# Self attention's weight preparation moved into the tile network's routing: a blind prediction and its test

## The reference, cut to what matters

```python
q = where(signatures_raw > 0.3, 1, where(signatures_raw < -0.3, -1, 0))
cluster_idx = argmax(calibrate(xf @ cluster_sigs.T, knots, temperature))
local_idx   = argmax(of the tile gates inside the chosen cluster)
comp = tanh(gelu(xf @ compress_w1 + compress_b1) @ compress_w2 + compress_b2)
```

```python
Q = (x @ Wq.T + bq)   # K and V alike; Wq is 1024 x 128
scores = Q K^T * (64 ** -0.5 * adaptive_scale) ; w = softmax(scores)
y = x + ((w V) @ Wo.T + bo)
y = (y - mean(y)) / sqrt(var(y) + 1e-5) * gamma + beta
```

## Time and profile before

| what | us |
|---|---|
| median of 3 runs | 1909.03 |
| the runs | 1909.03, 1908.49, 1919.20 |
| the profiled execution's own time | 1915.3 |
| its span, first to last instruction | 1913.4 |
| tile network's first matmul | at 997.81 |
| tile network's last write of xT ends | at 1135.48 |
| first projection of self attention | at 1150.75 |
| first scores of self attention | at 1170.50 |

### The profile page before, as it was taken

One profiled execution on the slowest core, in us unless ns is written; L12 is line 12 of the kernel. 1 busy time (PEld: TensorE's weight loads), 2 busy tenths in 40 slices (PEclk: granted clock), 3 DMA queues, 4 the chain that ended last, 5 costly groups with the idle time before them and its releaser, 6 DMA issues. The chain is left out here.

```text
span 1913.4 us, 28911 instructions
## 1 busy us (share of the span) xinstructions
PE 1666.6 (87%) x10515; PEld 952.9 (50%) x10515; DVE 1266.2 (66%) x1719; ACT 1204.2 (63%) x2565; POOL 478.5 (25%) x396
## 2 busy tenths in 40 slices
PE   5999999999999865888776878999999999589976
PEld 2344444444343322666654534656666666356655
DVE  2777777777777729798727444566666666388864
ACT  3787777777777624788862344555655556267764
POOL 2111011111111105777610001222222223145540
PEclk9999999999999955899985678999999999789997
DMA  3000000000000021000000000000000000000001
GB/s 127 1 12 1 1 6 24 0 0 0 0 0 1 0 47 30 5 5 8 2 2 0 1 0 1 1 1 1 1 1 1 1 1 1 7 8 8 2 1 45
DMA packets 30529, 16.99 MB, mean 9 GB/s; under 512 B 8545, under 2 KB 29246, under 8 KB 30398
## 3 DMA queue, kind: packets, MB, share of 16 engines
q1 hardware_dynamic: 27710, 10.52, 2.1%
q10 hardware_dynamic: 2688, 4.72, 0.7%
HBM read 13.14 MB, written 2.10 MB: 8 GB/s over the span
## 5 line engine op out<-in xcount | busy, mean ns | idle before, releaser
L2090 POOL TENSOR_TENSOR self_probs<-self_probs,self_rz 128x1024 f32<-128x1024 f32 x64 | 121.4, 1897 | 516.9 <-DVE self_rz L2118 516.9
L536 POOL TENSOR_SCALAR gru_decay<-gru_zgate 128x512 f32<-128x512 f32 x96 | 75.5, 786 | 570.0 <-ACT gru_zgate L489 544.0
L2065 ACT ACTIVATE self_probs<-self_scores,self_neg 128x128 f32<-128x128 f32 x512 | 181.8, 385 | 16.6 <-DVE self_neg L2113 16.6
L402 PE MATMUL gru_gate<-gru_xn,gru_whg 128*128 128x512 f32 x384 | 182.5, 598 | 3.5 <-DVE gru_xn L582 3.5
L406 PE MATMUL gru_hid<-gru_xn,gru_whg 128*128 128x512 f32 x384 | 181.3, 594 | 0.0
L414 PE MATMUL gru_out<-gru_y,gru_wo 128*128 128x512 f32 x384 | 178.1, 599 | 0.7 <-DVE gru_y L610 0.7
L1235 ACT ACTIVATE x_pt<-x_turned 77x512 f32<-77x512 f32 x256 | 137.4, 586 | 62.1 <-PE x_turned L1126 60.8
L1126 PE MATMUL x_turned<-const_ident,x_probs 128*77 128x128 f32 x1024 | 142.8, 283 | 24.0 <-POOL x_probs L1284 12.5
L1126 PEld LDWEIGHTS x_turned<-const_ident,x_probs 128*77 128x77 f32 x1024 | 115.3, 150 | 76.3 <-POOL x_probs L1284 27.1
L605 DVE SCALAR_TENSOR_TENSOR gru_ghid<-gru_hid,gru_half_c,gru_sighid 128x512 f32<-128x512 f32 x96 | 71.8, 747 | 114.8 <-ACT gru_sighid L490 114.6
L1359 DVE TENSOR_REDUCE x_m<-x_scores 128x16 f32<-128x1232 f32 x64 | 91.5, 1430 | 45.8 <-PE x_scores L1115 40.8
(11 more groups left out here) (377 smaller groups left out, 3567.9 us busy)
## 6 DMA issues: line engine op xcount, KB each, us to landing
gru_whg<-in_L_attn_Whg ACTq DMA_DIRECT2D x4, 768.0 KB, 9.2
x0e_ctx_in<-in_ctx SPq DMA_DIRECT2D x16, 154.0 KB
gru_xin<-in_x SPq DMA_DIRECT2D x8, 256.0 KB, 2.8
out<-moe_y SPq DMA_DIRECT2D x8, 256.0 KB, 2.3
gru_wo<-in_L_attn_Wo ACTq DMA_DIRECT2D x4, 384.0 KB, 10.3
selfe_raw<-in_L_attn_Wq SPq DMA_DIRECT2D x1, 512.0 KB, 4.3
selfe_raw<-in_L_attn_Wk SPq DMA_DIRECT2D x1, 512.0 KB, 5.5
selfe_raw<-in_L_attn_Wv SPq DMA_DIRECT2D x1, 512.0 KB, 6.7
```

Of the source, the lines that this page charges most:

```text
L402: mm(ps_gate[n % 2][:, :], whg[:, l, k, DI + c * P:DI + (c + 1) * P], xn[u][:, k, :], start=(k == 0), stop=(k == KH - 1))
L2065: last = f(probs[n % 2][:, a, jj, :], ps_s[n % 2][:, a, jj * T:(jj + 1) * T], ACT.Exp, bias=neg[n % 2][:, a, jj:jj + 1], accum_out=z[n % 2 ...
L2090: pool.tensor_tensor(probs[n % 2][:, :, :, :], probs[n % 2][:, :, :, :], whole, ALU.mult).then_inc(pn_ready.sem, 1)
```

## The change

The eight fills, the centring and the bias leave self attention and are written into the tile network's only block: on PE and ACT between the compress network and the loop, on POOL behind the iota. ACT makes all eight copies. The output weights are no longer transposed and then centred by DVE: PE multiplies each raw block by the constant centring matrix (1 - 1/128 on the diagonal, -1/128 elsewhere), which turns and centres in one matmul. The output bias is one accumulation group on PE (centring matrix times bo, then the eight one-column products), and ACT copies it. The vectors are scaled by POOL. The banks are the tile network's `norm` banks, which the Gelu was the last to read, and `centred1` for the bias. `turn_weights` and the second block are gone, so self attention begins with its main block.

```diff
+    def hold(self):
+        self.w = {n: self.t.sb(f"w_{n}", [P, INNER]) for n in "qkvo"}
+        self.fills = [(k, n, c) for k, n in enumerate("qkvo") for c in range(0, PAIRS, 4)]
+    def turn(self, pe, nc, const, bank, bias_bank):
+        pe.wait_ge(self.loaded.sem, self.n_loads * DMA)
+        for f, (k, n, c) in enumerate(self.fills):
+            if f >= 2:
+                pe.wait_ge(self.kept.sem, f - 1)
+            for j in range(4):
+                at, block = bank[f % 2][:, j * P:(j + 1) * P], self.raw[:, k, c + j, :]
+                if n == "o":
+                    last = nc.tensor.matmul(at, block, const["centre"][:, :], start=True, stop=True)
+                else:
+                    last = nc.tensor.transpose(at, block, const["ident"][:, :])
+            last.then_inc(self.turned.sem, 1)
+        pe.wait_ge(self.kept.sem, len(self.fills))
+        nc.tensor.matmul(bias_bank[:, 0:1], const["centre"][:, :], self.bo_c[:, :], start=True, stop=False)
+        for c in range(PAIRS):
+            last = nc.tensor.matmul(bias_bank[:, 0:1], self.w["o"][:, c * P:(c + 1) * P], self.bv_c[:, c:c + 1], start=False, stop=(c == PAIRS - 1))
+        last.then_inc(self.bias_mm.sem, 1)
+    def keep(self, act, nc, bank, bias_bank):
+        for f, (k, n, c) in enumerate(self.fills):
+            act.wait_ge(self.turned.sem, f + 1)
+            nc.scalar.activation(self.w[n][:, c * P:(c + 4) * P], bank[f % 2][:, :], ACT.Copy).then_inc(self.kept.sem, 1)
+        act.wait_ge(self.bias_mm.sem, 1)
+        nc.scalar.activation(self.bo_c[:, :], bias_bank[:, 0:1], ACT.Copy)
+    def scale(self, pool):
+        pool.wait_ge(self.loaded.sem, self.n_loads * DMA)
+        pool.tensor_scalar(self.sc_c[:, :], self.sc_c[:, :], HD ** -0.5, None, ALU.mult).then_inc(self.scaled.sem, 1)
+        pool.wait_ge(self.scaled.sem, 1)
+        pool.tensor_tensor(self.bq_c[:, :], self.bq_c[:, :], self.sc_c[:, :], ALU.mult)
-def turn_weights(nc, const, tag, pairs, bank, loaded, n_loads):
...
             def _(pool):
                 pool.iota(iota_i[:, :, :], pattern=[[0, B], [1, TPC]], base=0, channel_multiplier=0).then_inc(iota_made.sem, 1)
+                own.scale(pool)
...
                 compress(NG - 1)
+                own.turn(pe, nc, const, ps_n, ps_z[1])
                 pe.wait_ge(dirs_ready.sem, 1)
...
                 f(e3, mine[:, :, :], ACT.Exp, scale=nit[:, :]).then_inc(exp_done.sem, 1)
+                own.keep(act, nc, ps_n, ps_z[1])
...
-        turn_weights(nc, const, "self_w", [(w[n], early.raw[:, k, :, :]) for k, n in enumerate("qkvo")], ps_t, early.loaded, early.n_loads)
...
-        with nc.Block() as block:
...
-                nc.tensor.matmul(bank[0][:, 0:1], const["mean"][:, :], bo_c[:, :], start=True, stop=True).then_inc(bias_mm.sem, 1)
-                pe.wait_ge(centred_w.sem, 1)
...
-                nc.vector.tensor_reduce(mid[:, :], wo_by_block, AX.X, ALU.add).then_inc(scaled.sem, 1)
...
-                nc.vector.tensor_tensor(bo_c[:, :], bo_c[:, :], bank[1][:, 0:1], ALU.add)
```

More of the change, by code:

```diff
@@ L825, in __init__ @@
         self.n_loads = 4 + len(self.vectors)
+        self.turned = t.count("turned")
+        self.kept = t.count("kept")
+        self.scaled = t.count("scaled")
+        self.bias_mm = t.count("bias_mm")
+    def hold(self):
[29 more added lines that the diff above has]
+        pool.tensor_tensor(self.bq_c[:, :], self.bq_c[:, :], self.sc_c[:, :], ALU.mult)
     def load(self, sp):
@@ L1443, in tile_ffn, with tile_ffn_stage @@
     const["stages"].append(arguments)
-def tile_ffn_stage(nc, const, early, xT):
+def tile_ffn_stage(nc, const, early, own, xT):
     with ExitStack() as ctx:
@@ L1810, in self_attention_stage @@
         LAST = NG * STEPS
-        w = {n: t.sb(f"w_{n}", [P, INNER]) for n in "qkvo"}
+        w = early.w
         bq_c, bk_c, bv_c, sc_c = early.bq_c, early.bk_c, early.bv_c, early.sc_c
         bo_c, gamma_c, beta_c = early.bo_c, early.gamma_c, early.beta_c
-        mid = t.sb("mid", [P, PAIRS])
         ps_s = [t.ps(f"scores{r}", [P, 2, 512]) for r in range(2)]
@@ L1832, in self_attention_stage @@
         sq, logs, inv = (spare[:, r * GROUP:(r + 1) * GROUP] for r in range(2, 5))
-        scaled = t.count("scaled")
-        bias_mm = t.count("bias_mm")
-        centred_w = t.count("centred_w")
-        with nc.Block() as block:
-            @block.tensor
-            def _(pe):
-                pe.wait_ge(early.loaded.sem, early.n_loads * DMA)
-                nc.tensor.matmul(bank[0][:, 0:1], const["mean"][:, :], bo_c[:, :], start=True, stop=True).then_inc(bias_mm.sem, 1)
-                pe.wait_ge(centred_w.sem, 1)
-                for c in range(PAIRS):
-                    last = nc.tensor.matmul(bank[1][:, 0:1], w["o"][:, c * P:(c + 1) * P], bv_c[:, c:c + 1], start=(c == 0), stop=(c == PAIRS - 1))
-                last.then_inc(bias_mm.sem, 1)
-            @block.vector
-            def _(dve):
-                wo_by_block = w["o"][:, :].rearrange("p (c d) -> p c d", d=D)
-                nc.vector.tensor_reduce(mid[:, :], wo_by_block, AX.X, ALU.add).then_inc(scaled.sem, 1)
-                dve.wait_ge(scaled.sem, 1)
-                nc.vector.tensor_scalar(mid[:, :], mid[:, :], 1.0 / D, None, ALU.mult).then_inc(scaled.sem, 1)
-                dve.wait_ge(scaled.sem, 2)
-                nc.vector.tensor_tensor(wo_by_block, wo_by_block, mid[:, :].unsqueeze(2).broadcast_to([P, PAIRS, D]), ALU.subtract).then_inc(centred_w.sem, 1)
-                dve.wait_ge(early.loaded.sem, early.n_loads * DMA)
-                nc.vector.tensor_scalar(sc_c[:, :], sc_c[:, :], HD ** -0.5, None, ALU.mult).then_inc(scaled.sem, 1)
-                dve.wait_ge(scaled.sem, 3)
-                nc.vector.tensor_tensor(bq_c[:, :], bq_c[:, :], sc_c[:, :], ALU.mult)
-                dve.wait_ge(bias_mm.sem, 2)
-                nc.vector.tensor_tensor(bo_c[:, :], bo_c[:, :], bank[0][:, 0:1], ALU.subtract).then_inc(scaled.sem, 1)
-                dve.wait_ge(scaled.sem, 4)
-                nc.vector.tensor_tensor(bo_c[:, :], bo_c[:, :], bank[1][:, 0:1], ALU.add)
         turned = [t.count(f"turned{e}") for e in range(2)]
```

3 lines of the change are left out of this document (2 added, 1 removed).

## The result

| | median of runs (us) | lowest to highest | profiled execution | its span |
|---|---|---|---|---|
| before | 1909.24 (4 runs) | 1908.49 to 1919.2 | 1915.3 | 1913.4 |
| changed | 1889.44 (4 runs) | 1889.15 to 1892.61 | 1889.31 | 1887.6 |

The ratio of the times is 0.9906, 95% interval 0.9879 to 0.9934: about 18 us less. The medians differ by 19.8 us, and the spans of the two profiled executions by 25.8, because before's profiled execution (1915.3) was 6 us above its own median and this one is at it.

The account below looks back on a forecast made before the run. DVE's chain was taken to bound the routing, and the weight preparation ahead of the projections to lie wholly on the path. Removal 14.5, routing 0 and the opening's middle gave -15.3 from 1909.0: 1893.7 us, range 1889.0 to 1900.0.

Parts of the forecast that it names:

- The removed piece: Between tile network and first projection: turning, centring, bias and their barriers go, 14.52 us, leaving 0.75 us of barrier and clear.
- The new work in the routing: PE and ACT work ahead of the first one-hot turn: hidden by DVE's second calibration, cost 0, bounds 0 to +2.3 us.
- Rival 2: Routing overruns: PE reaches the first turn up to 2.3 us late; gain 13.0, about 1896 us; chance 0.07.
- POOL's two operations: Two 128x8 operations behind POOL's iota: cost 0, bound +0.9 us if both stand in DVE's way.
- The opening: Self attention's 18 projections and value products: 1.85 us gained if the clock stays 1.00, none with one short low stretch.
- Rival 1: Opening cold for long: a low stretch of 7 to 10 us; gain only 11.3 to 12.9, about 1897 us; chance 0.18.
- Rival 3: Tile loop starts at full clock, up to 9.4 us less there; gain up to 24.7, 1884.3 us; chance 0.06.
- The sum: Whole kernel: 15.3 us saved, taken from the median of 1909.0, giving 1893.7 us.
- what follows them: Sign listed in advance: the span of everything behind the scores stays unchanged.
- if the tile loop changes its length by more than 2 us: Sign of being wrong: the loop from first turn to last write, 78.8 us, was expected to keep its length.
- DVE's chain bounds this stretch: Routing: PE idles 19.16 us until DVE's one-hot, with PE and ACT both free.
- Rival 4: Tile loop's clock stays low: +26 us less 15.3 saved, 1919.8 us; chance 0.05, beyond the 15.3 only 0.02.

Follow-up runs that it names:

- e7: Changed kernel with only the 32 transposes moved to the routing; centring, bias and scaling stay in their old block ahead of self attention. 0.9965 of before.
- e4: Kernel before with the routing's new PE and ACT work added, the old blocks kept and POOL's two operations left out. 1.0009 of before.
- e3: Changed kernel without turning, centring or bias; POOL fills the four weights with a constant instead. 0.9951 of before, 1895.46 us.
- e11: Changed kernel with one more POOL fill of 128x1024, read by nobody, behind POOL's two small operations. Single run, 1898.44 us.
- e5: Changed kernel without PE's new routing work; ACT copies the raw weights straight, the bias stays as loaded. 0.9912 of before, 1889.93 us.
- e6: Changed kernel with seven unread 512-column matmuls on PE behind the bias, ahead of the first turn. 0.989 of before.
- e9: Changed kernel with eight unread 512-column matmuls behind the bias and one more inside the loop ahead of the first weighed turn. 0.9871 of before, 1882.87 us.
- e2: Changed kernel run and traced a second time, no edit. 0.9918 of before.
- e8: Changed kernel run and traced a third time, no edit. 0.9903 of before, 1887.36 us.
- e10: Changed kernel with seven unread 512-column matmuls behind the bias, the same kernel as e6 run again. 0.9895 of before.
- e1: Kernel before run and traced a second time, no edit. 0.9996 of before.

## Why the prediction was right, and where it was not

**The removed piece, -14.5.** Right: 15.27 to 0.75 against the trace that the term was read from. The gap was 0.75 in all nine traces without the old blocks, and 15.3 to 16.1 in all three with both, so the piece is worth 14.5 to 15.4; the forecast had the lower end, from the one trace there was. Its halves are 7.5 (turning) and 7.0 (centring and bias), by e7.

**The new work in the routing, 0.** Right, by 7.7 to 7.9 us of idle PE behind it, and e4's 1.0009 does not speak against it. Rival 2 is out. The slack was mis-sized: I had 4.2 us for PE and 4.6 for ACT; they were 7.85 and 8.72. I had put all of it at the low clock; the centring took 1.55 us less than that and the 18 one-column matmuls some 1.85, which is 3.4 of the 3.65 us. The clock rose at the end of the transposes, to 0.74 and then 1.00:

```profile
1036.00:1038.00 2.00, 2.00 (x14) 1.63 (x13) 1.86 (x5) 1.41 (x3) 0.00 (x0) 0.74 0.00 0
1038.00:1040.00 2.00, 1.31 (x13) 1.12 (x11) 1.93 (x7) 1.20 (x2) 0.00 (x0) 1.00 0.00 0
```

PE did nothing but 128x128 transposes from 1033.6 to 1037.3, and matmuls of that size behind them. In e7, where all 32 blocks are transposes (24 of them from 1041.10 to 1046.22, nothing else on PE), it is plainer still:

```profile
1043.00:1045.00 2.00, 2.00 (x11) 1.63 (x11) 1.83 (x6) 1.29 (x3) 0.00 (x0) 0.50 0.00 0
1045.00:1046.20 1.20, 1.13 (x8) 0.66 (x6) 1.13 (x4) 1.10 (x2) 0.00 (x0) 1.00 0.00 0
```

The rule weighed in the prediction (the Trainium skill, "TensorE: Matmul & The Clock Gate", section "PE-mode transpose": transposes do not count as busy for the clock) is contradicted here as it was by the earlier trace rows.

**POOL's two operations, 0, bound +0.9.** Right: DVE's rows beside them keep their 0.20 to 0.23 us. The bound had a real mechanism behind it, which e3 and e11 priced.

**The opening, -1.7 to 0, I took the middle.** Both cases occurred; the cold one was mis-sized, at -0.65 us (19.75 to 19.1) where I had 0. In the traces that go from the tile network straight to the projections it took 17.96 or 17.97 five times (changed, e5, e6, e9, e11) and 19.07 to 19.12 four times (e2, e3, e8, e10). A short low stretch in four of nine, and no long one. PE in e2, and the clock there:

```profile
1127.30 2.05 PE L1959 MATMUL self_bank<-xT,selfe_w_q 128*128 128x512 f32 x2 [3.10 <-PEq L84]
1129.14 1.57 PE L1959 MATMUL self_bank<-xT,selfe_w_k 128*128 128x512 f32 x2
1130.54 1.02 PE L1959 MATMUL self_bank<-xT,selfe_w_q 128*128 128x512 f32 x2
```
```profile
1124.20:1126.80 2.60, 0.00 (x1) 0.00 (x0) 1.38 (x2) 1.59 (x3) 0.00 (x0) 1.00 0.00 0
1126.80:1127.30 0.50, 0.00 (x0) 0.03 (x1) 0.00 (x0) 0.04 (x1) 0.00 (x0) 0.52 0.00 0
1127.30:1130.20 2.90, 2.90 (x4) 1.15 (x4) 0.00 (x0) 2.02 (x2) 0.00 (x0) 0.50 0.02 6
```

Rival 1 (3.5 to 5.1 us lost) was in none of the nine. That a gap sends the array back to half clock (the same page of the Trainium skill, "Why this matters for your kernels") is half borne out. In e2, e8 and e10 the clock fell inside the gap ahead of the projections, with PE idle for 2.6 us and more, as the rows of e2 show; in e3 it fell 1.4 us into the projections. In the other five it did not fall at that gap. The changed kernel's first trace, idle for 3.2 us there:

```profile
1120.00:1124.30 4.30, 1.14 (x3) 0.30 (x3) 1.38 (x2) 2.53 (x5) 0.00 (x0) 1.00 0.00 0
1124.30:1142.30 18.00, 17.76 (x37) 5.70 (x38) 6.00 (x8) 8.09 (x10) 0.00 (x0) 1.00 0.00 1
```

**Rival 3's reason.** I expected the low clock at the first turn because one-column matmuls come last, and read from the earlier trace rows that the clock went down under them. It had gone down before: between 1144 and 1146 PE was busy for 0.11 us, and the 16 began at 1146.50. In the changed kernel they ran at full clock (1.93 us) and the clock fell in the idle time behind them. The low clock at the first turn came as forecast, but it followed the idle time and not these matmuls; e6, e9 and e10 filled that idle time with wide matmuls and had the full clock there.

**The sum.** Gap and opening together are 35.0 us in before and 35.9 in e1, and 18.7, 19.9 and 19.8 in the three traces of the changed kernel: 15.2 to 17.2 us less. Three measurements of the changed kernel, by their ratios, gave 17.9, 15.6 and 18.5 us (by their medians 19.8, 16.5 and 20.2). Each interval holds the forecast's 15.3. That the first time fell inside the range is in part luck: it was 0.4 us from the edge, and the third median of the same kernel, 1887.36, lies outside. Taking the saving from the median and not from the profiled span helped, since the profiled execution of before was longer than its median. The spans differ by 25.8, and by the table these are 14.5 gap, 1.8 opening, 3.1 routing, 5.2 loop, 3.6 ahead of the stage and -2.4 behind it. The last four change between two executions of one kernel as well.

**What failed.** Several of the signs listed in advance did not come as written: PE's idle ahead of the first turn was 7.85 us and not about 4, the first turn came 6.7 us earlier and not at the same time, the scores 28.2 us earlier and not 15 to 16, and what follows them was 2.4 us longer. And "if the tile loop changes its length by more than 2 us" was offered as a sign that the reasoning was wrong. It changed by 5.2, and the reasoning on the removed piece stood. The slack apart, these signs failed for one reason: they took the pieces of one execution for properties of the kernel. The loop of the changed kernel is 73.6 to 75.7 from execution to execution, of the one before 75.7 to 78.8; the routing 55.8 or 58.9 with not a line changed. The step "DVE's chain bounds this stretch" is true from the exponential on; ahead of it, in the trace that I had, a PE at 0.59 of its clock (compress end 39.70) was the bound.

**What stays open.** Whether the changed kernel meets the cold pattern less often. Its three traces have routing 55.79 each; before's have 58.86 and 55.79, those of e4 and e7 64.73, that of e11 59.67. Its loops of 73.6 to 75.7 meet before's 75.7 to 78.8 only at one end, and two traces of before are too few to say that it can have 73.6 as well. The measured 15.6 to 18.5 reaches a little above the 15.2 to 17.2 that gap and opening explain, with intervals of some 5 us to either side, and the untouched kernel's runs spread over 19 us. Many more traces of each would be needed; not tried. Rival 4, the loop staying cold, did not occur in the changed kernel; e11, with a 78.81 loop, is as near as any trace came, and before had that too.

## What to carry to other kernels

Work that stands alone between two barriers is worth its whole length when it moves beside a chain that another engine sets (here 14.5 to 15.4 us, as its own length varied); look for the engine that idles, and work out the slack at the low clock, where it is smallest. Before a difference of a few microseconds in a stage is explained, profile the unchanged kernel a second time: here 8 of the 26 us between two spans lay in a routing and a loop whose lengths differ between executions of one kernel. Where PE idles ahead of a dense stretch, a few unread wide matmuls in the idle time can hand it a fast clock, but as soon as PE is fast the neighbours set the pace, and about half of the promised gain was all that came (3 traces, loops of 70.0 to 72.2 us against 73.6 to 75.7).

## What the runs showed of the hardware that I had not expected

- While POOL filled, a DVE operation that started beside the fill did not end before it: 0.20 us became 1.00 beside one 128x1024 fill of 0.95 us (e11), and 3.68 beside four in a row (e3). POOL's small arithmetic (0.24 and 0.20 us on 128x8) left its neighbours at 0.20 to 0.23.
- The compress network, the same instructions in the same order and hardly a gap in PE, ran at full clock from its second piece nearly to its end in eight of the 13 traces (1.05 us for each piece, done 33.7 us into the stage, 37.3 in e3) and at the low clock throughout in two (e4 and e7: 1.92 and 1.86, done after 45.6). No run was made to find what decides it. One thing goes with it: the clock had fallen 4.8 to 5.3 us before the stage's first matmul in the nine traces that were soon fast again, and 5.7 to 6.5 us before it in the other four (before, e4, e7, e11). The low clock in e4, with PE busy throughout:

```profile
995.70:1038.50 42.80, 42.78 (x145) 29.55 (x145) 24.84 (x57) 9.28 (x17) 0.00 (x0) 0.50 0.00 1
```

- The same gap of 3.1 to 3.2 us in PE had two outcomes in one kernel: the clock stayed at 1.00 in the changed kernel's first trace and fell before the gap's end in e2 and e8. In the 7.85 us of idle ahead of the first turn it fell too: 0.61 on average, and 0.50 for the tile loop that opens behind it. With dense 512-column matmuls in that idle time (e9) it stayed at 0.99.
